# Ternary feed-forward: input and inner rows turned by DMA transposes in the tile loop instead of by TensorE, down-projection two tiles behind

## The reference

```python
def act_quant(x):
    scale = 127.0 / jnp.clip(jnp.max(jnp.abs(x), axis=-1, keepdims=True), EPS)
    return jnp.clip(jnp.round(x * scale), -128.0, 127.0) / scale

def bitlinear(x, w):
    return jnp.einsum('bsd,hd->bsh', act_quant(x), weight_quant(w))

h = jax.nn.silu(bitlinear(x, w1)) * bitlinear(x, w3)
return bitlinear(h, w2)
```

## Time and profile before

| | |
|---|---|
| median of 3 runs | 1227.72 us (1226.38 to 1228.2) |
| span of the profiled execution | 1223.2 us |
| busy share of the span | PE 91%, DVE 69%, ACT 42%, POOL 33% |
| granted TensorE clock, mean | 0.964 |
| tile loop of the ternary stage | about 261 to 420 us of the span |
| busy in 261.4 to 422.0 | PE 133.2, DVE 118.3, ACT 97.7, POOL 15.4 us |

### The profile page before, as it was taken

One profiled execution on the slowest core, in us unless ns is written; L12 is line 12 of the kernel. 1 busy time (PEld: TensorE's weight loads), 2 busy tenths in 40 slices (PEclk: granted clock), 3 DMA queues, 4 the chain that ended last, 5 costly groups with the idle time before them and its releaser, 6 DMA issues. The chain is left out here.

```text
span 1223.2 us, 22308 instructions
## 1 busy us (share of the span) xinstructions
PE 1108.5 (91%) x6266; PEld 835.1 (68%) x6284; DVE 845.2 (69%) x1628; ACT 511.3 (42%) x1067; POOL 402.8 (33%) x323
## 2 busy tenths in 40 slices
PE   6999799978888599999989997999999999999997
PEld 5989676544444257898878664776777776777773
DVE  3548447878886655787887994767677677666646
ACT  1332134266666247888722162333333333333330
POOL 0000001111110020466764001556666556566630
PEclk9999899999999898998989997999999999999999
DMA  7324330010000058765156413878789898778659
GB/s 263 146 109 163 127 131 1 0 19 1 0 0 1 35 178 282 259 240 189 45 198 222 82 52 120 233 188 219 181 228 246 197 235 224 185 186 190 140 98 378
DMA packets 98716, 183.29 MB, mean 150 GB/s; under 512 B 13513, under 2 KB 31305, under 8 KB 98672
## 3 DMA queue, kind: packets, MB, share of 16 engines
q1 hardware_dynamic: 81040, 144.41, 35.1%
q0 software_dynamic: 17632, 38.32, 15.9%
HBM read 136.56 MB, written 50.34 MB: 153 GB/s over the span
## 5 line engine op out<-in xcount | busy, mean ns | idle before, releaser
L2377 POOL DMA_INDIRECT y_d<-tail,x_ox x78 | 167.3, 2144 | 134.5 <-ACT tail L2604 105.4
L2449 PE MATMUL x_h<-x_w_hi,x_t_hi 128*128 x320 | 127.9, 400 | 2.3 <-DVE x_t_lo L2618 2.3
L2450 PE MATMUL x_h<-x_w_lo,x_t_hi 128*128 x320 | 127.7, 399 | 0.0
L2451 PE MATMUL x_h<-x_w_hi,x_t_lo 128*128 x320 | 127.4, 398 | 0.0
L1662 POOL DMA_INDIRECT e_rows<-r_d,x_ix x80 | 85.0, 1063 | 125.2 <-issue 107.8
L2618 DVE TENSOR_TENSOR x_w_lo<-w,x_w_hi (+1 forms) x64 | 109.6, 1753 | 2.6 <-ACT x_w_hi L2575 2.6
L2566 ACT ACTIVATE e_rows<-x_h 128x256 f32<-128x256 f32 x80 | 30.8, 384 | 184.0 <-PE x_h L2451 184.0
L211 POOL TENSOR_TENSOR ln_rstd<-ln_ve,powers 128x2 f32<-128x2 f32 (+1 forms) x40 | 26.2, 655 | 245.6 <-DVE ln_ve L205 245.6
L2618 DVE TENSOR_TENSOR x_t_lo<-x_xb,x_t_hi 128x512 fp32r<-128x512 f32 x80 | 55.2, 692 | 42.2 <-ACT x_t_hi L2561 42.2
L1542 DVE SCALAR_TENSOR_TENSOR h_c<-h_qk,h_d 128x768 f32<-128x768 f32 x64 | 58.2, 952 | 26.2 <-PE h_qk L1436 14.4
L2468 PE MATMUL x_o<-x_w_hi,x_avt_hi 128*128 x160 | 71.5, 447 | 1.6 <-issue 1.3
(11 more groups left out here) (435 smaller groups left out, 2667.4 us busy)
## 6 DMA issues: line engine op xcount, KB each, us to landing
w<-in_L_ffn_w SPq DMA_DIRECT2D x32, 1024.0 KB, 7.7
w<-in_L_ffn_w SPq DMA_DIRECT2D x32, 512.0 KB, 9.8
h_negm<-negm_d SPq DMA_DIRECT2D x15, 1024.0 KB, 6.9
raw<-in_L_ffn_w SPq DMA_DIRECT2D x3, 2816.0 KB, 16.3
x_res<-in_x SPq DMA_DIRECT2D x8, 512.0 KB, 4.7
ctx_in<-in_ctx SPq DMA_DIRECT2D x8, 512.0 KB, 3.7
kt_d<-ct SPq DMA_DIRECT2D x8, 512.0 KB, 3.1
vc_d<-ctx_in SPq DMA_DIRECT2D x8, 512.0 KB, 2.6
```

Source lines behind the costliest of these rows:

```text
L2377: nc.gpsimd.indirect_dma_start(out=y_d[s], out_offset=bass.IndirectOffsetOnAxis(ap=ox[q][:, s:s + 1], axis=0), in_=eo[q][s][:], in_offset= ...
L2449: nc.tensor.matmul(hbank[s], hi[:, k, :], w13p[0][:, at, k, :], start=k == 0, stop=False)
L2450: nc.tensor.matmul(hbank[s], hi[:, k, :], w13p[1][:, at, k, :], start=False, stop=False)
L2451: last = nc.tensor.matmul(hbank[s], lo[:, k, :], w13p[0][:, at, k, :], start=False, stop=k == KD - 1)
```

## The change

`f_xq`, `f_hq` and `f_hqt` get two buffers each. PE no longer turns rows, ACT no longer copies them: SP issues one DMA transpose for each tile's `f_xq` (128 x 512 bf16, 128 KB) and one for each tile's `f_hq` (128 x 1408 bf16, 352 KB), each of which waits for the integers and for the last reader of its destination. `down` of t-2 stands between g and u of tile t, and its result goes to `turn_a` and `turn_b` in turn. The hardware loop covers 8 tiles instead of 10.

```diff
+        def turn_x(t, par):
+            sp.wait_ge(xq_ready, t + 1)
+            after(sp, u_ps, t - 1)
+            sp.dma_start_transpose(xqt[:, par], xq[:, par]).then_inc(xqt_in[par], 16)
+        def turn_h(t, par):
+            sp.wait_ge(hq_ready, t + 1)
+            after(sp, o_ps, t - 1)
+            sp.dma_start_transpose(hqt[:, par], hq[:, par]).then_inc(hqt_in[par], 16)
+        for t in range(NT + 1):
+            if t:
+                turn_h(t - 1, (t - 1) % 2)
+            for ahead in range(3) if t == 0 else (t + 2,):
+                if ahead < NT:
+                    turn_x(ahead, ahead % 2)
...
-        def down(t):
-            pe.wait_ge(hta_sb, t + 1)
-            pe.wait_ge(htb_sb, t + 1)
+        def down(t, par, m):
+            pe.wait_ge(hqt_in[par], 16 * m + 16)
+            after(pe, x_added, t - 1)
...
-        def tile(t, par):
-            first = isinstance(t, int) and t == 0
-            pe.wait_ge(xqt_sb, t + 1)
+        def tile(t, par, m):
+            inner = not isinstance(t, int)
+            pe.wait_ge(xqt_in[par], 16 * m + 16)
             after(pe, sil_ready, t)
-            up(par, g_bank, w1t, g_ps, range(3))
-            more = not isinstance(t, int) or t + 1 < NT
-            if more:
-                turn_x(t + 1)
+            up(par, g_bank, w1t, g_ps)
+            if inner or t >= 2:
+                down(t - 2, par, m - 1)
             after(pe, u_used, t)
-            up(par, u_bank, w3t, None, range(2))
-            if not first:
-                if more:
-                    pe.wait_ge(xqt_sb, t + 2)
-                turn_h(t - 1)
-            up(par, u_bank, w3t, u_ps, range(2, 3))
-            if not first:
-                down(t - 1)
+            up(par, u_bank, w3t, u_ps)
...
-        def integers_h(t):
+        def integers_h(t, par, m):
             dve.wait_ge(ha_ready, t + 1)
-            after(dve, htb_ps, t)
-            integers(hq, hid, hq_ready)
+            after(dve, hqt_in[par], 16 * m)
+            integers(hq[:, par], hid, hq_ready)
```

More of the change, by code:

```diff
@@ L689, in bit_ffn @@
     d13 = sbuf(st, "f_d13", [P, 2, 2])
-    xq = sbuf(st, "f_xq", [P, D], BF16)
+    xq = sbuf(st, "f_xq", [P, 2, D], BF16)
     xqt = sbuf(st, "f_xqt", [P, 2, KD, P], BF16)
@@ L693, in bit_ffn @@
     hid = sbuf(st, "f_hid", [P, F0])
-    hq = sbuf(st, "f_hq", [P, F0], BF16)
-    hqt = sbuf(st, "f_hqt", [P, KF, P], BF16)
+    hq = sbuf(st, "f_hq", [P, 2, F0], BF16)
+    hqt = sbuf(st, "f_hqt", [P, 2, KF, P], BF16)
     hbig = sbuf(st, "f_hbig", [P, 1])
@@ L707, in bit_ffn @@
     KA = 8
+    o_bank = [ta, tb]
     nmr = sbuf(st, "f_nmr", [P, 1])
@@ L717, in bit_ffn @@
     early_in = sem("f_early_in")
-    (round_ready, nmean_ready, nmr_ready, xn_ready, xs_ready, xa_ready, d_ready, xq_ready, xqt_ps, xqt_sb, g_ps, u_ps, sil_ready, u_used,
-     hs_ready, ha_ready, hq_ready, hta_ps, htb_ps, hta_sb, htb_sb, o_ps, x_added) = (
+    (round_ready, nmean_ready, nmr_ready, xn_ready, xs_ready, xa_ready, d_ready, xq_ready, g_ps, u_ps, sil_ready, u_used,
+     hs_ready, ha_ready, hq_ready, o_ps, x_added) = (
         sem("f_" + n) for n in ("round_ready", "nmean_ready", "nmr_ready", "xn_ready", "xs_ready", "xa_ready", "d_ready", "xq_ready",
-                                "xqt_ps", "xqt_sb", "g_ps", "u_ps", "sil_ready", "u_used", "hs_ready", "ha_ready",
-                                "hq_ready", "hta_ps", "htb_ps", "hta_sb", "htb_sb", "o_ps", "x_added"))
+                                "g_ps", "u_ps", "sil_ready", "u_used", "hs_ready", "ha_ready",
+                                "hq_ready", "o_ps", "x_added"))
+    xqt_in, hqt_in = ([sem(f"f_{n}_in{u}") for u in range(2)] for n in ("xqt", "hqt"))
     jobs = []
@@ L742, in tiles @@
     def tiles(eng, first, middle, last):
[L744 to L748, removed]
+        for t in range(4):
+            first(t, t % 2, t // 2)
+        with eng(0, NT // 2 - 4) as i:
+            for u in range(2):
+                middle(2 * i + 4 + u, u, i + 2)
         for t in range(NT - 4, NT):
-            last(t, t % 2)
+            last(t, t % 2, t // 2)
     @block.sync
@@ L809, in _, with up @@
             pe.wait_ge(wt_sb[e], (len(jobs) + 1 - e) // 2)
[L811 to L818, removed]
+        def up(par, bank, wgt, done):
+            for n in range(3):
                 lo, hi = 512 * n, min(512 * n + 512, F0)
@@ L822, in up, with tile @@
                                             start=k == 0, stop=k == KD - 1)
[L823 to L828, removed]
-            for k in range(KF):
[L830 to L833, removed]
-        def down(t):
-            pe.wait_ge(hta_sb, t + 1)
-            pe.wait_ge(htb_sb, t + 1)
-            for k in range(KF):
-                last = nc.tensor.matmul(ta[:], hqt[:, k, :], w2t[:, k, :], start=k == 0, stop=k == KF - 1)
+            last.then_inc(done, 1)
+        def down(t, par, m):
+            pe.wait_ge(hqt_in[par], 16 * m + 16)
+            after(pe, x_added, t - 1)
+            for k in range(KF):
+                last = nc.tensor.matmul(o_bank[par][:], hqt[:, par, k, :], w2t[:, k, :], start=k == 0, stop=k == KF - 1)
             last.then_inc(o_ps, 1)
-        def tile(t, par):
-            first = isinstance(t, int) and t == 0
-            pe.wait_ge(xqt_sb, t + 1)
+        def tile(t, par, m):
+            inner = not isinstance(t, int)
+            pe.wait_ge(xqt_in[par], 16 * m + 16)
             after(pe, sil_ready, t)
-            up(par, g_bank, w1t, g_ps, range(3))
-            more = not isinstance(t, int) or t + 1 < NT
-            if more:
-                turn_x(t + 1)
+            up(par, g_bank, w1t, g_ps)
+            if inner or t >= 2:
+                down(t - 2, par, m - 1)
             after(pe, u_used, t)
-            up(par, u_bank, w3t, None, range(2))
-            if not first:
-                if more:
-                    pe.wait_ge(xqt_sb, t + 2)
-                turn_h(t - 1)
-            up(par, u_bank, w3t, u_ps, range(2, 3))
-            if not first:
-                down(t - 1)
-        turn_x(0)
+            up(par, u_bank, w3t, u_ps)
         tiles(pe.Fori, tile, tile, tile)
-        turn_h(NT - 1)
-        down(NT - 1)
+        for t in range(NT - 2, NT):
+            down(t, t % 2, t // 2)
     @block.scalar
@@ L881, in grid_h @@
             nc.scalar.activation(hid[:], hid[:], ACT.Identity, bias=round_up[:], scale=hscl[:]).then_inc(ha_ready, 1)
-        def copy_x(t, par):
-            act.wait_ge(xqt_ps, t + 1)
-            nc.scalar.copy(xqt[:, par], tbb[:, 0:KD, :]).then_inc(xqt_sb, 1)
         def silu(t, par):
@@ L906, in tile @@
             silu(t, par)
-            if inner or t + 1 < NT:
-                copy_x(t + 1, 1 - par)
             if inner or t + 2 < NT:
                 grid_x(t + 2)
-            if inner or t:
-                copy_h(t - 1)
         def weight_copies(lo, hi):
@@ L928, in _ @@
         weight_copies(18, len(jobs))
-        copy_x(0, 0)
         grid_x(1)
@@ L932, in _ @@
         grid_h(NT - 1)
-        copy_h(NT - 1)
     @block.vector
@@ L946, in integers @@
         def integers(dst, src, done):
-            nc.vector.tensor_scalar(dst[:], src[:], ROUND, 127.0, ALU.subtract, ALU.min).then_inc(done, 1)
+            nc.vector.tensor_scalar(dst, src[:], ROUND, 127.0, ALU.subtract, ALU.min).then_inc(done, 1)
         def moments(t):
@@ L957, in spread_x, with integers_x @@
             spread(xn, big, deq[:, par:par + 1], scl, xs_ready)
-        def integers_x(t):
+        def integers_x(t, par, m):
             dve.wait_ge(xa_ready, t + 1)
-            after(dve, xqt_ps, t)
-            integers(xq, xn, xq_ready)
+            after(dve, xqt_in[par], 16 * m)
+            integers(xq[:, par], xn, xq_ready)
         def hidden(t, par):
@@ L981, in residual, with tile @@
             row = x[:, ds(t, 1), :]
-            nc.vector.scalar_tensor_tensor(row, ta[:], hd2[:, par:par + 1], row, ALU.mult, ALU.add).then_inc(x_added, 1)
-        def tile(t, par):
+            nc.vector.scalar_tensor_tensor(row, o_bank[par][:], hd2[:, par:par + 1], row, ALU.mult, ALU.add).then_inc(x_added, 1)
+        def tile(t, par, m):
             inner = not isinstance(t, int)
@@ L989, in tile @@
             if inner or t:
-                integers_h(t - 1)
+                integers_h(t - 1, 1 - par, m - 1 + par)
             if inner or t + 2 < NT:
@@ L996, in tile @@
             if inner or t + 2 < NT:
-                integers_x(t + 2)
+                integers_x(t + 2, par, m + 1)
         def weight_copies(lo, hi):
@@ L1010, in _ @@
         weight_copies(10, 16)
-        integers_x(0)
+        integers_x(0, 0, 0)
         weight_copies(16, len(jobs))
@@ L1014, in _ @@
         moments(2)
-        integers_x(1)
+        integers_x(1, 1, 0)
         tiles(lambda lo, hi: steps.loop(lo, hi, 14), tile, tile, tile)
         steps.settle()
+        integers_h(NT - 1, 1, NT // 2 - 1)
         residual(NT - 2, 0)
-        integers_h(NT - 1)
```

## The result

The changed kernel takes **1211.75 us** (median of 4, 1209.05 to 1214.84) against 1227.39 us beside it: ratio 0.9879, 95% interval 0.9851 to 0.9907, 15.6 us faster. The forecast was 1218.5 us and a range of 1209 to 1269; the direction and the place were right, the size was that of a rival. A few executions took far longer than the others of their kernel (1268.92 us of order, 5864.87 of xdma, 1591.41 of the kernel before beside mixed); medians and ratios here are without them. The profiled execution took 1214.45 us with a span of 1212.7. In the changed kernel `up` is L836, `down` L844, `hidden` L948, the integers L927, `residual` L962, `grid_h` L877, `silu` L883.

The account below looks back on a forecast made before the run. The loop was taken to be bound by a ring ending in DVE's wait for PE's u. Start -0.4, steps -11.1 and end +2.3 sum to -9.2 us, giving a median of 1218.5 us, range 1209 to 1269.

Parts of the forecast that it names:

- The bound before: Old loop: a ring where DVE makes h, PE turns it inside u, DVE waits for u's end; 9.3 us a tile.
- The floor of 8.34 us: Loop: shortest tile step once DVE no longer waits for u, set by DVE and ACT; 1.0 us under now.
- The ring 4.26 + Lh: Loop: down, residual, f_hq, h's transpose, next down, one tile long; under the floor up to Lh = 4.1 us.
- Lh = 4.4 us: h's DMA transpose, integers to semaphore: 4.4 us, taken from the m_wraw load as nearest in count of pieces.
- rival 1: Loop: transposes as quick as copies, Lh under 4.1, steps at the floor; -18 to -15.5 us, 1211 us; chance 0.18.
- the likeliest case: Loop: Lh from 4.1 to 5.0, its ring setting the pace; 1210 to 1227 us, chance 0.32.
- One of its signs: Profile after: PE idle 1.4 us a tile before down, DVE idle 0.3 us before x_res for PE, among others.
- 11 of them go one after another: h's transpose: 11 blocks in series, Lh = 14.2, ring 18.5 us a tile, +138 us, 1366 us; chance 0.12.
- Steps: Loop, between DVE's scales of tiles 0 and 15: 128.5 us against 139.6, minus 11.1.
- The end: From the scale of tile 15 on: 11.9 us against 9.6, plus 2.3, with down at the halved clock, 4.05 us.
- The start: Tile 0: g and u come over 1 us earlier, then silu is the next that is late; minus 0.4 us.
- Rival 5, the clock: PE in the loop: busy share falls to 82%, half clock, three groups need 14.2 us a tile; +72 us, 1300; chance 0.03.

Follow-up runs that it names:

- order: Kernel before, PE and ACT keeping turns and copies; down of t-2 between g and u, f_hqt two buffers, copy_x ahead of normal: 1215.80 us, ratio 0.9930.
- xdma: Kernel before with only x turned by SP's DMA; h still turned by PE inside u, down of t-1 at the tile's end: 1216.07 us, ratio 0.9928.
- mixed: Changed kernel with h turned by PE in the middle of u and copied by ACT, x still by DMA: 1204.10 us, ratio 0.9826.
- order2: As order, against the kernel before, but copy_x stands between normal and silu on ACT; no DMA transposes: 1209.02 us, ratio 0.9872.
- light: Changed kernel taking the inner row's largest value over 704 of 1408 columns, so it computes something else: 1201.90 us, ratio 0.9810.
- ring: Changed kernel with an extra 512-column transpose of f_hq issued and awaited before each tile's h transpose: 1242.46 us, ratio 1.0136.
- the repeat: The changed kernel run again unaltered, as neighbour for other runs on the same chip: 1211.18 us, ratio 0.9894.
- Tail: Changed kernel with h of the last two tiles turned by PE into the banks of g and u and copied by ACT: 1207.16 us, ratio 0.9845.
- xlast: Changed kernel with SP issuing x of t+2 behind h of t instead of ahead of it: 1282.18 us, ratio 1.0466.

## Why the prediction was right in direction and short in size

- *The bound before*: right. DVE waited for u, u waited in PE's list. Shown from both sides by xdma and order2. That the loop is a ring that ends in DVE's wait for u was too narrow: a step was PE's list of one tile with its waits for the copies, 9.35 us.
- *The floor of 8.34 us*: right, measured 8.44; the 0.1 lies between ACT's end and `f_hq` (334.04 to 334.18, before 347.00 to 347.03), where the wait for the buffer's transpose is new. In mixed that wait is one for PE, and the gap is 0.03 again (336.21 to 336.24); this speaks for the wait as the cause, though no run changes it alone. That the floor is DVE's and ACT's, light shows.
- *The ring 4.26 + Lh*: right to 0.1 us at 10.4 (ring), at 8.0 (light, 7.9 by the sum) and in the last two steps (7.77 and 7.82).
- *Lh = 4.4 us*: **the term that was mis-sized.** It is 3.6 (16 transposes, median), so the ring lies under the floor and rival 1 is what happened, which had 0.18 beside my 0.32. That 1211.75 also lies in the likeliest case's 1210 to 1227 is no support for that case: its ring did not set the pace. One of its signs came all the same, DVE idle 0.26 us before `x_res` for PE, and so does not tell the two apart; the other, PE idle 1.4 us before `down`, did not come. The count of pieces was right: a stretch that holds one h transpose has 1440 packets, 1408 of them rows of 256 bytes by the count. Its packets and the share of the 16 queues in 2.2 us:

```profile
DMA packets 1440, 0.36 MB, mean 164 GB/s; under 512 B 1440, under 2 KB 1440, under 8 KB 1440
...
q1 hardware_dynamic: 1440, 0.36, 85.4%
```

  16 x 2.2 x 0.854 / 1440 = 20.9 ns a packet, 1.9 us for h, 1.7 fixed. The same two terms give 1.7 + 512 x 20.9 ns / 16 = 2.4 us for x, as measured. I had carried over the load from HBM, whose 3.6 us hold 96 x 10.4 ns = 1.0 us of packets a queue and 2.6 us of fixed time; that reading from HBM "rather makes it long" I wrote, and put no number on it. The Trainium skill (Advanced Engine Details and Errata, X-Bar Transpose (TRN2)) puts transposing DMAs level with regular ones. The trace does not agree: h moves at 360,448 bytes / 1.9 us = 190 GB/s against 381, half of that. The rule's outcome (the floor) came true all the same, since 1.7 and 1.9 us together stay under the slack of 4.1. The Trainium skill (VectorE: DVE Perf Modes, The three transpose paths) gives 1309 ns for one 128 x 128; that 11 of them go one after another, 14.4 us by this estimate, is excluded by the measured 3.6.
- *Steps*: 128.5 predicted, 125.3 measured, 121.9 in rival 1. The 3.4 us over rival 1: 2.2 in the first twelve steps, 1.2 in the last three, where h's ring holds. In the first twelve, 1.2 belong to the second step, 9.50 us, where a g of 12 matmuls took 4.22 us after a gap of 2.55 at a granted clock of 0.58; the repeat has 8.24 there. Another 0.3 lie in the fifth step (8.68 us, in the repeat 9.05), at full clock: h's transpose issued at 300.79 took 4.6 us to land instead of 3.6 (4.9 in the repeat), `down` waited 1.12 us for it and DVE 0.91 for `down`. Packets of the instruction queues moved during both; that they held the transpose up was not tested.
- *The end*: +2.3 predicted, +2.2 measured, by luck: Lh with its gaps was 3.6 instead of 4.5, and the last `down` took 4.87 us instead of the 4.05 carried over from before, since the clock stayed at the half all through it (0.62 in the mean before). The two errors, 0.9 and 0.8, cancel. Tail takes 1.9 back.
- *The start*: -0.4 predicted. From the first turn of a weight to the scale of tile 0 it is 23.0 us against 23.2 before, and 21.4 in the repeat and five other runs that turn x by DMA. Where it is 23.0, PE's last turns of the weights ran partly at the half clock (granted 0.59 in 256.0 to 260.2 us), as they did before (0.57 in 254 to 258); in the repeat the clock there was 1.00. So the start varies by 1.6 us with the clock, more than the term.
- *Rival 5, the clock*: not in the steady loop (granted 1.00), but real at its start, its end, in two tiles of ring, and in xlast.

## What to carry to other kernels

Look for the shortest ring that a new latency enters, not for the number of tiles by which the consumer is set back: here `residual` ahead of `integers_h` on DVE closed it within one tile, and the slack was 4.1 us, not two tiles. Ask separately what the order gives and what the new unit gives, stretch by stretch: here moving `down` between g and u was enough for the whole gain in the loop. Moving 15 turns a tile to the DMA engines added nothing to that. H's transposes cost 2 us at the end; x's saved 3 us at the start against order2, and the fastest kernel, mixed, turns x by DMA and h on PE. And in a queue with one order, such as SP's, a transfer must not stand behind one that waits for something later (xlast: 70 us).

## What the runs showed of the hardware

A DMA transpose out of SBUF into SBUF landed 2.4 us (128 x 512 bf16) and 3.6 us (128 x 1408; 3.5 to 4.6 over the 16) after its issue, and kept SP for 1.19 and 1.26 to 1.38 us each, so two a tile take 2.5 of 8.4 us of its queue. Packets of 256 bytes took 20.9 ns in it, those of 64 bytes in a load 10.4. In the ring run PE has one gap of about 3 us a tile. The granted clock was 1.00 behind most of them (340 to 360 us), but 0.69 in the `down` behind the one at 370 us, which at 3.04 us was no longer than the others. In xlast, with one gap of 3.7 to 4.0 us a tile, it was 0.74 in the mean of 300 to 380 us: g ran at 0.50 behind the gap and u at 1.00 again.
